# First attention stage: one order for all engines, written by an event plan over its 32 groups

## The reference

```python
x = x + attn_a(layernorm(x))      # dense causal attention, the stage changed here
x = x + ffn(layernorm(x))         # gated, with blockwise FP4 rounding
x = x + attn_b(layernorm(x))      # sparse attention with rotary positions
x = x + ffn(layernorm(x))

def attn_a(x):                    # x: 8 x 1024 x 256, 16 heads of 16
    Q, K, V = split(x @ W_qkv.T + b_qkv)
    scores = einsum('bhqd,bhkd->bhqk', Q, K) / sqrt(16) + causal
    O = einsum('bhqk,bhkd->bhqd', softmax(scores), V)
    return O @ W_o.T + b_o
```

## Time and profile before

| | us |
|---|---|
| median of 3 runs (3417.87 to 3424.49) | 3421.76 |
| the profiled execution | 3419.68 |
| its span, first to last instruction | 3417.9 |
| PE, PEld busy in the span | 3138.9, 2110.1 |
| DVE, ACT, POOL busy in the span | 2614.7, 1730.4, 1130.2 |
| first maxima of the stage (DVE) | 263.2 |
| last output copy of the stage (ACT) ends | 1177.7 |

### The profile page before, as it was taken

The page is one execution under the profiler, slowest core; times in us unless marked ns, Lnnn a source line. Parts: engine busy times, 40 slices in busy tenths (PEclk is TensorE's granted clock), DMA queues, the critical chain, the costliest instruction groups (busy, mean ns, idle before and its releaser), DMA issues. The chain is left out here.

```text
span 3417.9 us, 92654 instructions
## 1 busy us (share of the span) xinstructions
PE 3138.9 (92%) x34732; PEld 2110.1 (62%) x34828; DVE 2614.7 (76%) x5407; ACT 1730.4 (51%) x3363; POOL 1130.2 (33%) x1888
## 2 busy tenths in 40 slices
PE   4988999999999799999997969999999979999999
PEld 2655666666666467777774535555555547777776
DVE  6548888888888589999986976556565648999997
ACT  3654667667777533333334644555555543333333
POOL 2542222222222222222224663444444432222222
PEclk9997999999999899999998989999999989999999
DMA  3764333333332122222214664544444422222221
GB/s 113 237 206 103 87 87 87 87 95 89 94 91 75 54 82 85 84 88 86 83 62 156 199 194 108 115 113 103 101 115 115 97 65 80 85 85 88 85 83 56
DMA packets 390676, 351.82 MB, mean 103 GB/s; under 512 B 111814, under 2 KB 331846, under 8 KB 390214
## 3 DMA queue, kind: packets, MB, share of 16 engines
q1 hardware_dynamic: 390342, 347.10, 37.3%
HBM read 210.12 MB, written 135.27 MB: 101 GB/s over the span
## 5 line engine op out<-in xcount | busy, mean ns | idle before, releaser
L814 DVE TENSOR_REDUCE aA_nmax<-bank 128x1 f32<-128x512 f32 (+3 forms) x1216 | 713.4, 656 | 136.3 <-PE bank L881 82.9
L853 ACT ACTIVATE aA_prob<-bank 128x512 f32<-128x512 f32 (+1 forms) x1216 | 599.0, 589 | 226.6 <-PE bank L906 224.2
L875 PE MATMUL bank<-aA_ks,aA_qs 96*32 96x512 bf16 (+14 forms) x6144 | 476.1, 324 | 42.6 <-DVE aA_nmax L814 21.9
L1219 DVE TENSOR_REDUCE aB_nmax<-bank 128x2 f32<-128x512 f32 (+1 forms) x512 | 325.1, 657 | 204.5 <-PE bank L1313 105.1
L906 PE MATMUL bank<-aA_qs,aA_ks 99*32 99x512 bf16 (+11 forms) x6144 | 460.5, 317 | 17.0 <-DMA aA_qs<-aA_rows 14.2
L1282 ACT ACTIVATE aB_prob<-bank 128x512 f32<-128x512 f32 (+1 forms) x512 | 271.5, 572 | 134.4 <-PE bank L1313 130.4
L875 PEld LDWEIGHTS bank<-aA_ks,aA_qs 96*32 96x32 bf16 x6144 | 228.0, 96 | 153.9 <-DVE aA_nmax L814 117.4
L925 PE MATMUL bank<-aA_prob,aA_vq 128*32 128x512 f32 (+3 forms) x3072 | 320.7, 489 | 0.0
L906 PEld LDWEIGHTS bank<-aA_qs,aA_ks 99*32 99x32 bf16 x6144 | 211.3, 96 | 145.0 <-issue 59.0
L797 POOL TENSOR_TENSOR aA_spare<-aA_spare 128x1 f32<-128x1 f32 x256 | 49.4, 193 | 711.2 <-ACT aA_prob L853 711.2
L1313 PE MATMUL bank<-aB_ks,aB_qs 96*128 96x256 bf16 (+3 forms) x2048 | 245.1, 258 | 38.8 <-DMA aB_own<-own_d 28.6
(11 more groups left out here) (242 smaller groups left out, 6642.2 us busy)
## 6 DMA issues: line engine op xcount, KB each, us to landing
parts_A<-pA_part SPq DMA_DIRECT2D x96, 256.0 KB, 3.3
aA_qs<-parts_A SPq DMA_DIRECT2D x192, 128.0 KB
aA_ks<-parts_A SPq DMA_DIRECT2D x192, 128.0 KB
parts_B<-pB_part SPq DMA_DIRECT2D x96, 256.0 KB, 2.6
aB_qs<-parts_B SPq DMA_DIRECT2D x192, 128.0 KB
aB_ks<-parts_B SPq DMA_DIRECT2D x192, 128.0 KB
o_A<-aA_o_sb SPq DMA_DIRECT2D x32, 512.0 KB, 3.2
o_B<-aB_o_sb SPq DMA_DIRECT2D x32, 512.0 KB, 3.1
```

The lines of the kernel that those rows point to most:

```text
L814: nc.vector.tensor_reduce(dst, src, AX.X, ALU.max, negate=True).then_inc(s["max_taken"], 1)
L853: nc.scalar.activation(dst, src, ACT.Exp, scale=SCALE).then_inc(s["exp_done"], 1)
L875: ins = nc.tensor.matmul(out[32 * j:32 * j + 32, 0:w], qs[g][0:KROWS, h, q * P + 32 * j:q * P + 32 * j + 32], ks[g][0:KROWS, h, k0:k0 + w] ...
L1219: nc.vector.tensor_reduce(dst, src, AX.X, ALU.max, negate=True).then_inc(s["max_taken"], 1)
```

## The change

- `dense_order` and its per-group loop go. `dense_tasks()` writes down every unit of all 32 groups for every engine, with a cost, what it must come after, a rank (`at`, in groups) and the ring it uses. `plan()` runs through these as events: the engine that can start first takes, of the tasks that are ready, the one with the lowest rank. It gives each engine's whole order and the bank of each unit.
- M of group n may run up to 1.4 groups ahead of n by its rank, and is held back by T of n - 2 alone.
- TensorE waits for GpSimd's fills before its first unit, where before it waited after the first group's T.
- Each PV raises `pv_done` (before only those of the second half). The output is copied in two halves (`out`), each when its own half is complete; PV of half c of the next group waits for that half's copy.
- `PROBS` goes from 4 to 5. GpSimd's dummy operation and its wait for its own earlier work go.
- SP keeps its order of DMAs; its store waits for both halves.

By this plan TensorE's order in the middle of the stage, from E0 of group n to E0 of group n + 1, is as follows. A stroke marks the units of n + 1, two strokes those of n + 2, and o PV those of n - 1.

The diff, cut to its core:

```diff
+PV_UNITS = sorted(LAST_EXP)
+HALF_DONE = [PV_UNITS.index((3, 0)), PV_UNITS.index((7, 1))]
+PROBS = 5
+DENSE_BANKS = {"e": 3, "m": 3}
+def plan(tasks, hop, banks):
...
+    for _ in range(len(tasks)):
+        now, eng = min((max(free[e], min(map(from_when, keys))), e) for e, keys in open_.items() if keys)
+        key = min((k for k in open_[eng] if from_when(k) <= now), key=lambda k: tasks[k][3])
+        open_[eng].remove(key)
+        _, cost, _, _, line = tasks[key]
+        free[eng] = end = now + cost
+        order[eng].append(key[1:])
...
+            ready[u] = max(ready[u], end + (0 if tasks[u][0] == eng else hop))
...
+def dense_tasks():
...
+        put("sp qk", "qk", 0, 12000, -2, ("pe", "pv", n - RING, N_PV - 1))
+        put("sp v", "v", 0, 5000, -1, ("pe", "pv", n - 2, N_PV - 1))
+        for i, (heads, q, k0, kw, _) in enumerate(MAX_UNITS):
+            cols, at = len(heads) * kw, -1.4 + i / len(MAX_UNITS)
+            diag = k0 + kw == (q + 1) * P
+            put("pe", "max", i, 0.42 * cols + (20 * len(heads) if diag else 0) + 5, at, ("sp qk", "qk", n, 0),
+                ("dve", "turn", n - 2, 0), line="m")
+            put("dve", "max", i, 1.04 * cols + 85, at, ("pe", "max", n, i), line="m")
+        put("dve", "fold", 0, 100, -0.3, ("dve", "max", n, len(MAX_UNITS) - 1))
+        put("pe", "turn", 0, 200, -0.3, ("dve", "fold", n, 0), line="m")
+        put("dve", "turn", 0, 1450, -0.3, ("pe", "turn", n, 0), line="m")
+        put("sp rows", "rows", 0, 3500, 0, ("dve", "turn", n, 0))
...
+                put("pe", "pv", j, 1.67 * w + 40, at + 0.4, ("sp v", "v", n, 0), ("act", "exp", n, i),
+                    ("pool", "clear", n, k), *([("act", "out", pre, c)] if k == 0 else []))
...
+DENSE_PLAN, DENSE_SEQ = plan(dense_tasks(), 250, DENSE_BANKS)
...
-                    sp.wait_ge(s["o_copied"], b * NG + g + 1)
+                    sp.wait_ge(s["out_done"], 2 * n + 2)
...
-                            pool.wait_ge(s["diag_cleared"], upto(b, g, QT, k - 1))
-                        nc.gpsimd.tensor_tensor(spare[:, k % 2:k % 2 + 1], spare[:, 2:3], spare[:, 2:3], ALU.add)
...
+                for kind, n, i in DENSE_PLAN["dve"]:
+                    pieces[kind](n, i)
...
-                    act.wait_ge(s["pv_done"], (n + 1) * QT)
-                    nc.scalar.activation(o_sb[g % 2][:, :], ps_o.rearrange("p c t -> p (c t)"),
-                                         ACT.Copy).then_inc(s["o_copied"], 1)
+                def out(n, c):
+                    act.wait_ge(s["pv_done"], n * N_PV + HALF_DONE[c] + 1)
+                    if n >= 2:
+                        act.wait_ge(o_stored[n % 2], n // 2 * 16)
+                    nc.scalar.activation(o_sb[n % 2][:, c * 4 * P:(c + 1) * 4 * P], ps_o[:, c, :],
+                                         ACT.Copy).then_inc(s["out_done"], 1)
...
+                pe.wait_ge(s["ones_set"], RING + 2)
+                pieces = {"max": max_unit, "turn": turn_max, "exp": exp_unit, "pv": pv}
+                for kind, n, i in DENSE_PLAN["pe"]:
+                    pieces[kind](n, i)
```

More of the change, by code:

```diff
@@ L604, with from_when @@
 EXP_UNITS = exp_units()
-N_MAX = len(MAX_UNITS) + 1
-N_EXP = len(EXP_UNITS)
 LAST_EXP = {kc: max(i for i, u in enumerate(EXP_UNITS) if u[0:2] == kc) for kc in {u[0:2] for u in EXP_UNITS}}
+PV_UNITS = sorted(LAST_EXP)
+HALF_DONE = [PV_UNITS.index((3, 0)), PV_UNITS.index((7, 1))]
+N_PV = len(PV_UNITS)
+PROBS = 5
+RING = 4
+DENSE_BANKS = {"e": 3, "m": 3}
+def plan(tasks, hop, banks):
+    never = float("inf")
+    users = {key: [] for key in tasks}
+    for key, task in tasks.items():
+        for k in task[2]:
+            users[k].append(key)
+    waiting = {key: len(task[2]) for key, task in tasks.items()}
+    ready = {key: 0.0 for key in tasks}
+    free, order, open_ = {}, {}, {}
+    for key, task in tasks.items():
+        free[task[0]], order[task[0]] = 0.0, []
+        open_.setdefault(task[0], set())
+        if not task[2]:
+            open_[task[0]].add(key)
+    made, taken = {line: [] for line in banks}, {line: [] for line in banks}
+    def from_when(key):
+        eng, line = key[0], tasks[key][4]
+        if not line:
+            return ready[key]
+        if eng != "pe":
+            return ready[key] if made[line][len(taken[line])] == key[1:] else never
+        n = len(made[line]) - banks[line]
+        if n >= len(taken[line]):
+            return never
+        return max(ready[key], taken[line][n] + hop if n >= 0 else 0)
+    for _ in range(len(tasks)):
[5 more added lines that the diff above has]
+        order[eng].append(key[1:])
+        if line and eng == "pe":
+            made[line].append(key[1:])
+        elif line:
+            taken[line].append(end)
+        for u in users[key]:
+            waiting[u] -= 1
+            ready[u] = max(ready[u], end + (0 if tasks[u][0] == eng else hop))
+            if not waiting[u]:
+                open_[tasks[u][0]].add(u)
+    return order, {line: {key: i for i, key in enumerate(keys)} for line, keys in made.items()}
@@ L608 @@
 BANKS = 3
[L609 to L616, removed]
 def weave(streams, eaten, hop, clearing):
@@ L645, in weave @@
     return order
[L648 to L666, removed]
```

457 lines of the change are left out of this document (225 added, 232 removed).

## The result

The changed kernel takes 3339.79 us in the median (3336.09 to 3342.74) against 3421.66 us: 0.9759 of the time, 95% interval 0.9747 to 0.9771, faster. The forecast was 3325 us with a range of 3303 to 3366.

The account below looks back on a forecast made before the run. VectorE never gets free of TensorE's program order, at 27.72 us a group. The new period, 23.9 + 0.5 + 0.2 = 24.6 us, with start and tail ends the stage at 1081.1 us, 96.6 less: forecast 3325 us, range 3303 to 3366.

Parts of the forecast that it names:

- Start (8): Stage start: TensorE waits for all fills; first reduce moves from 263.20 to about 267.1 us, first exponents from 291.1 to 298.3.
- Maxima ahead (1): Group edge: later groups' maxima keep VectorE fed, removing its 1.48 and 0.45 us idle and TensorE's 0.54 us wait.
- Rows (2): Row DMA before a group's exponents: rows land 5.2 to 7.4 us after the transpose; 0.2 us charged, against 1 us now.
- Rival B: Row DMA stuck behind the period's 13 loads, so exponents wait and the kernel is slower: 3432 us, chance 0.03.
- the store and the loads (7): SP queue: the store waits for the second half, 13 load issues behind it; queue free about 14 us in, no cost.
- Coupling (3): Products spread among maxima with VectorE's three-bank ring: slack 0.5 us; 0.5 us a group charged, 0 to 1.9.
- Rival A: TensorE and VectorE still wait for each other, or TensorE is nearer full: period 25.8 us, 3362 us, chance 0.16.
- Rival C: VectorE, with its own pauses at fold and cut, is the bound: period 25.3 us, 3347 us, chance 0.10.
- Buffers, halves, dummy (4 to 6): Five probability buffers, halved output copies (up to 0.2 us more, hidden), GpSimd's dummy operation gone: no gain or cost charged.
- TensorE's floor: TensorE's work per group: 23.4 us of columns and transpose plus 0.5 for small diagonal matmuls, 23.9 us (23.4 to 24.3).
- End (9): Stage tail after the last reduce: 30 us, ScalarE-bound at 28.1 with the last products behind, against 28.3 us now.
- rival D: Small mask matmuls start at least about 25 ns apart: 1.9 us in all, period 26.5 us, 3384 us, chance 0.01.

Follow-up runs that it names:

- e1: Changed kernel, planned so that a later group's maxima may not cross the group edge; order inside the group still free: 3379.58 us, 0.9871 of the kernel before.
- e5: Changed kernel with every engine's unit order put back to that of the kernel before, all other parts kept: 3426.23 us, 1.0008 of the kernel before.
- e8: Changed kernel with each maximum taken over half of its columns, relieving VectorE with TensorE's work the same: 3324.76 us, 0.9709 of the kernel before.
- e2: Changed kernel with four probability buffers instead of five, planned anew: 3340.35 us, 0.9756 of the kernel before.
- e3: Changed kernel with one whole output copy a group instead of two halves: 3343.81 us, 0.9768 of the kernel before.
- e4: Changed kernel with GpSimd's dummy operation and its wait put back before each diagonal clearing: 3348.74 us, 0.9775 of the kernel before.
- e12: Changed kernel with no mask matmuls in the maxima pass and each maximum over half of its columns: 3286.52 us, 0.9598 of the kernel before.
- e10: Changed kernel with TensorE's wait for GpSimd's fills moved to just before the first exponent unit: 3339.52 us, 0.9755 of the kernel before.
- e6: Changed kernel with q and k loaded for one head of four from group 4 on, same number of DMAs: 3331.22 us, 0.9733 of the kernel before.
- e7: Changed kernel without the mask matmuls in the maxima pass, same order and waits: 3307.97 us, 0.9658 of the kernel before.

## Why the prediction was right, and by how much it missed

The direction, the place and the mechanism were right, and the time lies in the range, 15 us above the forecast. By its own steps:

- **Start (8).** First reduce 267.6 (forecast 267.1), first exponent matmul 298.31 (298.3). Right.
- **Maxima ahead (1).** Right, and e1 and e5 show it: without the edge's share 41.3 us are gone, without the order all of it. VectorE's idle time before maxima is 63.6 - 23.75 = 39.9 us over 31 groups, 1.3 us each instead of 3.6; with the first it is above the "under 50 us" of the prediction, and without it below.
- **Rows (2).** 0.2 us was charged for late rows; it is nothing. The tile of the row cut in after:

```profile
  PE bank L936: 0.9, 1
...
DMA to landing us min/median/max: 1.8/1.9/3.3
```

The 14.6 us in 32 waits are one wait of 0.9 us. The third row lands 4.5 to 6.4 us after the transpose, the exponents begin 6.0 us after it or later (5.7 in the last group), and the 33.4 us are at most 0.4. The prediction had 5.2 us as the least: it added the third issue's 0.6 us to a landing time that is counted from that issue's start. There is little to spare all the same: in nine groups the row lands less than half a microsecond before the first exponents, in two of them 0.04 or 0.05. Rival B fell: the store and the loads (7) do not delay the rows.
- **Coupling (3).** 0.5 us was charged, 0 to 1.9; it is 0, since e8, with VectorE at 63%, has the same 24.57 us. Rival A had 25.8 us and fell. Rival C named VectorE as the bound at 25.3; 24.91 lies near it in number, but e8 shows that VectorE's pauses set nothing.
- **Buffers, halves, dummy (4 to 6).** Nothing, as said for the buffers (e2). For the halves it was nothing in whole time, 0.4 us a group in the trace (e3). For the dummy operation nothing is shown (e4).
- **TensorE's floor.** Forecast 23.9 (23.4 to 24.3), measured 24.57 in e8: the term that was mis-sized, with the true value outside its bounds. 23.4 were the columns at full width. For masks I had 0.026 us a head over the full width from the earlier trace rows, 0.8 us for 32 heads, and took 0.5 because the trims were to "give part back". The 0.24 against 0.22 us above, 0.02 a head, is near that 0.026 and already has the trims of its unit in it, so hardly anything more was to be given back: about 0.3 us lost by that choice. The other 24.57 - 23.4 - 0.8 = 0.37 us was in no term. Most of it is the pitch of a full unit, which I took as 0.215 us from one pair in the earlier trace rows: over all units of 512 columns of one head from 400 to 1000 us in after and in e12, the median distance to the next unit's start is 0.219 or 0.220 us, which makes 72 x 0.0045 = 0.32 us. One pair of units was too short a stretch to read such a pitch from.
- **Pauses of TensorE.** Not foreseen: 24.91 - 24.57 = 0.34 us a group, 10.3 us over 30. The loads' traffic was costed only for what it does to the rows, not for what it does to the instructions of TensorE (last section).
- **End (9).** 31.4 us after the last reduce instead of 30.

The sum of the period is then 24.57 + 0 + 0 + 0.34 = 24.91 us, against 23.9 + 0.5 + 0.2 = 24.6. Two charges that turned out empty (0.7) made up for most of what was short or missing (0.67 + 0.34 = 1.01), so the 0.3 us of error looks better than the terms deserve. It is 9.4 us over 30 groups; with 1.9 us at the end the stage ends 11.4 us late. The other 4 us of the 15.4 are the second attention stage's 2.8 and about 1 in the others.

TensorE's busy share did mislead whoever read it as a limit. It was 25.74 of 27 us before, which as a floor gave 25.7 us and 3359. It is 593.7 of 600 us in after, and in e12 598.74 of 600 at a period 1.1 us shorter. The Trainium skill, "Perfetto Trace Analysis", section "Identifying the Most-Contended Engine", holds that matmul busy share is no good measure for TensorE; the trace agrees.

## What to carry to other kernels

Where two engines alternate through a program order, first ask what the later engine has to do at the edge of a group; here half of the gain came from letting it run over that edge and half from a finer interleaving inside, and none from buffers or copies alone. Read the pitch of the commonest unit over many of them, since 0.005 us on 72 units is a third of a microsecond, and test each floor by relieving the other engine: halving VectorE's work showed in one run that VectorE does not set the period. When an engine is brought to run without gaps, expect things to show that its waits had hidden, and expect an order tuned to one set of costs to fit another worse.

## What the runs showed of the hardware that was not expected

**TensorE runs out of instructions under DMA traffic.** In after, from 320 to 1060 us, ten distances between two matmul starts are over 0.5 us, 0.58 to 1.59. They lie 15 to 20 us after a group's first exponents, when the loads of q and k, issued from about 6 us after these on, are still being moved, and they come in a group or not. The page of after lists the queue that brings instructions (packets, MB, share of time):

```profile
q8 instruction: 242, 3.96, 0.5%
```

These are packets of 16 KB, and the trace has the start and length of each. From 320 to 1010 us there are 132 of them, and TensorE starts 33,782 matmuls and weight loads: one packet for 256. Each of the ten pauses ends 1.31 to 1.57 us after the end of such a packet, though one comes only every 5.2 us. And from the end of one pause to the end of the next TensorE starts 2559, 2305, 2559, 1280, 4608, 5121, 3584, 1279 and 6144 matmuls and weight loads, each within one of a multiple of 256. The 29 such pauses of e10, e2 and e8 end 1.23 to 1.55 us after a packet. So TensorE has come to the end of a packet's instructions, and the next packet is late.

What makes it late is the traffic: with a quarter of the loads and the same instructions (e6) no distance from 320 to 1010 us is over 0.5 us. The packets ahead of the ten pauses took 0.88 to 1.12 us, like the others (median 0.96), so it is their start that is late and not their transfer. It costs nothing where TensorE needs a packet less often: in e7 and e12, with the same traffic and a fifth fewer instructions, every 6.2 or 6.3 us instead of 5.2, and no such pause. In before, where TensorE waits for other things, it was every 5.8 us. Why e3, at 5.3 us, has only four such pauses stays open.

**The masks are dearer than they look.** The 128 mask matmuls of a group (4 for each of 32 heads) and their effect on the trimmed scores come to 1.13 us, 8.8 ns each, by e8 and e12. On four column strips such small matmuls start 10 ns apart (eight in 0.08 us). The Trainium skill, "TensorE: Matmul & The Clock Gate", section "Wait - 56ns, not 53.3ns?", has about 25 ns as the least distance, which as an estimate from that page makes 3.2 us for 128. The runs do not agree, and rival D fell with it.

**An unchanged stage varies.** The second attention stage took 758.5 us (e5) to 769.6 us (e8) with no edit to it, 11 us or 0.3% of the whole time. No experiment here says why; a difference below that between two kernels of this table is not read as an effect of the edit without the stage's own time beside it.
